# Layer 0 attention: paired maxima on row halves, and a step's values behind all its scores; layer 1's values at the end of the step

## The reference, cut to what matters

```python
# layer 0: 16 query heads of 64, 4 key/value heads, causal
q = (hidden_states @ Wq.T).reshape(B, S, 16, 64).transpose(0, 2, 1, 3)
k = (hidden_states @ Wk.T).reshape(B, S, 4, 64).transpose(0, 2, 1, 3)
v = (hidden_states @ Wv.T).reshape(B, S, 4, 64).transpose(0, 2, 1, 3)
k = jnp.repeat(k, 4, axis=1); v = jnp.repeat(v, 4, axis=1)
scores = jnp.einsum("bhqd,bhkd->bhqk", q, k) * scale + causal
probs = jax.nn.softmax(scores, axis=-1)
out = jnp.einsum("bhqk,bhkd->bhqd", probs, v)
return out.transpose(0, 2, 1, 3).reshape(B, S, 16 * 64) @ Wo.T
# layer 1's second attention: the same shape of work with 16 heads of 8, after a norm and rope
```

## Time and profile before

| | us |
|---|---|
| runs, median of 3 | 1522.89 (1521.58 to 1523.54) |
| the profiled execution | 1521.91 |
| its span, first to last instruction | 1520.2 |
| attention 64 | 43 to 640 |
| attention 8 | about 1006 to 1318 |

### The profile page before, as it was taken

One profiled execution on the slowest core, in us unless ns is written; L12 is line 12 of the kernel. 1 busy time (PEld: TensorE's weight loads), 2 busy tenths in 40 slices (PEclk: granted clock), 3 DMA queues, 4 the chain that ended last, 5 costly groups with the idle time before them and its releaser, 6 DMA issues. The chain is left out here.

```text
span 1520.2 us, 21410 instructions
## 1 busy us (share of the span) xinstructions
PE 1325.6 (87%) x7772; PEld 762.8 (50%) x7772; DVE 969.0 (64%) x1750; ACT 696.5 (46%) x1319; POOL 112.6 (7%) x155
## 2 busy tenths in 40 slices
PE   4689999999999999868999967337989888889998
PEld 3344444444444444346888845313334333256886
DVE  4556545454546462177999966748767655357998
ACT  2242434333333433244666654412665556525664
POOL 0000000101010101000000000302111111020000
PEclk9799999999999999959999979656999888868999
DMA  3101202020201110006676610041212210102221
GB/s 104 40 15 34 49 15 63 8 58 15 52 15 43 29 29 16 14 15 144 146 154 153 146 24 1 2 100 54 47 48 49 53 40 20 43 21 79 78 102 28
DMA packets 51475, 81.61 MB, mean 54 GB/s; under 512 B 16748, under 2 KB 34452, under 8 KB 47444
## 3 DMA queue, kind: packets, MB, share of 16 engines
q1 hardware_dynamic: 51004, 79.40, 21.2%
q10 hardware_dynamic: 384, 1.05, 0.6%
HBM read 63.75 MB, written 5.68 MB: 46 GB/s over the span
## 5 line engine op out<-in xcount | busy, mean ns | idle before, releaser
L1345 PE MATMUL ps<-qA 128*128 128x512 f32 x960 | 252.3, 399 | 15.3 <-POOL qA L1455 10.9
L634 DVE TENSOR_REDUCE mraw<-ps 128x1 f32<-128x512 f32 (+3 forms) x304 | 186.8, 656 | 108.7 <-PE ps L516 60.2
L736 ACT ACTIVATE shared<-ps 128x512 f32<-128x512 f32 (+1 forms) x216 | 121.3, 566 | 261.4 <-PE ps L549 259.8
L1062 DVE TENSOR_REDUCE mraw<-ps 128x2 f32<-128x1024 f32 (+3 forms) x160 | 173.5, 1114 | 78.0 <-PE ps L967 52.3
L1117 ACT ACTIVATE shared<-ps 128x512 f32<-128x512 f32 (+2 forms) x320 | 155.7, 560 | 136.6 <-PE ps L983 136.0
L1345 PEld LDWEIGHTS ps<-qA 128*128 128x128 f32 x960 | 182.5, 192 | 62.9 <-POOL qA L1455 12.3
L548 PE MATMUL ps<-qA,kH 128*128 128x512 f32 (+3 forms) x384 | 165.9, 442 | 6.1 <-DMA qB<-mT 5.8
L548 PEld LDWEIGHTS ps<-qA,kH 128*128 128x128 f32 x384 | 72.9, 190 | 150.7 <-issue 62.6
L1409 ACT CAST qA<-shared 128x512 fp32r<-128x512 f32 x160 | 99.3, 621 | 88.6 <-DVE shared L1547 87.0
L1357 PE MATMUL ps<-qA,kH 128*128 128x512 f32 x480 | 136.3, 393 | 4.0 <-DVE qA L1471 4.0
L549 PE MATMUL ps<-qB,kL 65*128 65x512 f32 (+3 forms) x384 | 130.5, 350 | 0.0
(11 more groups left out here) (247 smaller groups left out, 1755.2 us busy)
## 6 DMA issues: line engine op xcount, KB each, us to landing
shared<-comb SPq DMA_DIRECT2D x92, 256.0 KB, 4.3
qB<-qA SPq DMA_DIRECT2D x16, 512.0 KB, 4.8
rB<-a0rec_dram SPq DMA_DIRECT2D x60, 128.0 KB, 2.8
shared<-comb SPq DMA_DIRECT2D x7, 1024.0 KB, 4.4
rB<-a1rec_dram SPq DMA_DIRECT2D x28, 128.0 KB, 2.7
e0wUp<-in_w SPq DMA_DIRECT2D x48, 64.0 KB, 4.5
qA<-q_split SPq DMA_DIRECT2D x24, 128.0 KB
q_split<-qA SPq DMA_DIRECT2D x4, 512.0 KB
```

Of the source, the lines that this page charges most:

```text
L634: nc.vector.tensor_reduce(out[:, h0:h0 + n_h, qt % 4], src, AX, ALU.max).then_inc(w_free, 1)
L736: nc.scalar.activation(probs(n)[:, hs[0]:hs[-1] + 1, lo:512], src, ACT.Exp, scale=scale)\
L1062: nc.vector.tensor_reduce(out[:, :, js[0]:js[-1] + 1, qt % 4], src, AX, ALU.max).then_inc(x_free, 1)
L1345: ins = nc.tensor.matmul(bank[0:M, :], w[par][:, at:at + M], h[:, cols], start=(r == 0), stop=(r == 2))
```

## The change

1. `max` jobs come in pairs. The query heads' high parts and remainders are written so that even heads have the high part in rows 0 to 63 of `qA` and odd heads in rows 64 to 127. A pair is two matmuls of 64 rows each, on the two halves of the rows, into two banks: only the high part of the queries takes part in the maxima. Masks follow, one for each bank, on all 128 rows. Jobs of 128 and 256 keys are now two jobs (two heads each) instead of one or two, so a group has 40 maxima jobs instead of 38, in 20 pairs. A pair enters when the job three before its second has been released.
2. The planner moves a pair as one, with weight 2.
3. A step's three rounds of values stand as one block behind all its scores and jobs.
4. `copy_q` is two DMAs, one for the even and one for the odd heads.
5. In attention 8, `values` stands at the end of every step.

```diff
     def max_jobs_of(qc):
...
-                n = 512 // keys_in(qt, ch)
-                out += [(qt, ch, h, n) for h in range(0, REP, n)]
+                if keys_in(qt, ch) <= 256:
+                    out += [(qt, ch, i, (i, i + 2)) for i in range(2)]
+                else:
+                    out += [(qt, ch, h % 2, (h,)) for h in range(REP)]
...
-        weights = [3 if job[0] == "proj" else 1 for job in jobs]
+        weights = [{"proj": 3, "max": 2}.get(job[0], 1) for job in jobs]
...
-        opens = m % NU in (0, 4)
+        behind = k - 1
...
-            upto = 3 if i == k - 1 else (i if opens else i + 1)
-            since = 0 if i == 0 else (i - 1 if opens else i)
-            rounds = range(min(since, 3), min(upto, 3)) if m >= 0 else ()
+            rounds = range(3) if m >= 0 and i == behind else ()
...
+                def maxima(pair):
...
+                    if pair[1] >= JOB_BANKS:
+                        pe.wait_ge(w_free, pair[1] - JOB_BANKS + 1)
...
+                    for slot, h in enumerate(evens):
+                        for i in range(2):
+                            half = slice(i * hd, (i + 1) * hd)
+                            ins = nc.tensor.matmul(k.bank(pair[i] % JOB_BANKS)[:, slot * width:(slot + 1) * width],
+                                                   k.qA[par][half, h + i, qt * P:(qt + 1) * P],
+                                                   k.kH[par][half, ch * 512:ch * 512 + width], start=(slot == 0),
+                                                   stop=not diagonal, skip_group_check=True)
...
-                    sp.dma_start(k.qB[g % 2][0:hd, :, cols].bitcast(F32), k.qA[g % 2][0:hd, :, cols].bitcast(F32))\
-                        .then_inc(qb_ld[qc], 16)
+                    for i in range(2):
+                        sp.dma_start(k.qB[g % 2][0:hd, i::2, cols].bitcast(F32),
+                                     k.qA[g % 2][i * hd:(i + 1) * hd, i::2, cols].bitcast(F32)).then_inc(qb_ld[qc], 16)
...
-                    between = n >= LAG and len(jobs) == 4 and (n - LAG) % NU not in (0, 4)
...
-                        if at == 1 and between:
-                            values(n - LAG)
-                    if n >= LAG and not between:
+                    if n >= LAG:
                         values(n - LAG)
```

More of the change, by code:

```diff
@@ L489, in _, with job @@
             def _(pe):
-                def job(idx):
+                def maxima(pair):
+                    kind, g, qc, j = JOBS[pair[0]]
+                    par = g % 2
+                    if pair[1] >= JOB_BANKS:
+                        pe.wait_ge(w_free, pair[1] - JOB_BANKS + 1)
+                    if j == 0:
+                        pe.wait_ge(w_free, index["proj", g, qc, U - 1] + 1)
+                    qt, ch, _, evens = MAXES[qc][j]
+                    width = keys_in(qt, ch)
+                    diagonal = ch * 512 + width == (qt + 1) * P
+                    n_h = len(evens)
+                    for slot, h in enumerate(evens):
[5 more added lines that the diff above has]
+                                                   stop=not diagonal, skip_group_check=True)
+                            if not diagonal and slot == n_h - 1:
+                                ins.then_inc(w_full, 1)
+                    if diagonal:
+                        for i in range(2):
+                            ends = k.bank(pair[i] % JOB_BANKS)[:, 0:n_h * width]\
+                                .rearrange("p (h w) -> p h w", w=width)[:, :, width - P:width]
+                            nc.tensor.matmul(ends, k.ident_bf[:, :], k.masks[:, 1:2, :].broadcast_to((P, n_h, P)),
+                                             start=False, stop=True, skip_group_check=True).then_inc(w_full, 1)
+                def job(group):
+                    if len(group) == 2:
+                        maxima(group)
+                        return
+                    idx = group[0]
                     kind, g, qc, j = JOBS[idx]
@@ L502, in job @@
                                          start=True, stop=True).then_inc(w_full, 1)
[L503 to L519, removed]
                     elif kind == "turn":
@@ L581, in values @@
                         ins.then_inc(pv_done, 1)
-                for idx in due[-1]:
-                    job(idx)
+                for group in due[-1]:
+                    job(group)
                 for n in range(STEPS + LAG):
@@ L588, in _ @@
                             scores(n, first_score[n] + at, hs)
-                        for idx in fills:
-                            job(idx)
+                        for group in fills:
+                            job(group)
                         for r in rounds:
@@ L596, in _ @@
                                      stop=True).then_inc(spread_full, 1)
[L597 removed]
+                job((index["fin", G - 1, 1, 0],))
             @block.vector
@@ L670, in normalise @@
                         .then_inc(on_done, 1)
-                for idx in due[-1]:
-                    take(idx)
+                for group in due[-1]:
+                    for idx in group:
+                        take(idx)
                 for n in range(STEPS + LAG):
@@ L681, in _ @@
                         (recips if at == 7 else normalise)(n // NU, 0)
-                    for idx in due.get(n, []):
-                        take(idx)
+                    for group in due.get(n, []):
+                        for idx in group:
+                            take(idx)
                 cols = slice(512, 1024)
@@ L818, in _ @@
                 load_out(1)
-                for idx in due[-1]:
-                    follow(idx)
+                for group in due[-1]:
+                    for idx in group:
+                        follow(idx)
                 for n in range(STEPS + LAG):
```

46 lines of the change are left out of this document (26 added, 20 removed).

## The result

| | before | after |
|---|---|---|
| runs, median (us) | 1523.21 (1521.58 to 1523.54) | 1546.78 (1541.94 to 1554.61) |
| ratio after to before | | 1.0162, 95% interval 1.0119 to 1.0205 |
| profiled execution, its span | 1521.9, 1520.2 | 1546.4, 1544.7 |
| first score of attention 64 | 57.0 | 60.9 |
| first group | 92.1 | 102.9 |

The changed kernel is 1.6% slower: 23.6 us by the medians, 24.5 by the two spans. The starts of a group's first score, and for the end the start of the matmul named, give the table, and they place the difference. Attention 64 is 35.1 us longer (start +3.9, first group +10.8, six steady groups +22.1, last group -1.8), attention 8 is 7.2 us shorter, the stages in between, in which nothing was changed, are 3.7 us shorter, and what follows attention 8 is 0.3 us longer.

The account below looks back on a forecast made before the run. TensorE's own queue was taken to bound layer 0's attention. From 1522 us, +20 for that stage and +10 for the clock gave 1552, put at 1550; range 1507 to 1570, likeliest case 1543 to 1562.

Parts of the forecast that it names:

- Item 5: Steps 4 and 5 of a steady group: second pair waits 1.7 us each on the projection's chain; +3.4 us a group.
- Item 6: Steps 6 to 9: pairs wait 0.2 to 0.3 us on the previous pair's reduce; +1.8 us a group.
- Items 1 to 4: TensorE's work in a steady group: values block -4.2, halved maxima -4.5, row-half visits +7.0, masks +0.1; -1.6 us.
- Item 8: Layer 0's attention: TensorE's clock falls behind half of 13 long waits; +10 us, bounds 0 and 22.
- The first group: First group of layer 0's attention: VectorE bounds its start and loses 0.3 us at each pair with masks; +3 us.
- item 7: Scores behind scores: in the last group the third head waits some 0.4 us in eight steps; +3.3 against -4.5.
- Item 9: Layer 1's attention: values move behind the fourth head in seven of 12 steps; 0 us, bounds -4 and +4.
- The chain doesn't bite: Rival: TensorE reaches the second pair no sooner than VectorE frees its bank; about 1507 us, chance 0.24.
- Pairs don't overlap: Rival: paired maxima don't overlap in layer 0's attention; +4.5 us a group, 1568 us; 0.08 shared with the every-wait clock fall.
- The half shape is free: Rival: row-half visits cost nothing but waits grow; +0.5 us a group, 1525 us, 1532 with the clock; chance 0.08.
- The clock holds: Rival: TensorE's clock doesn't fall behind the new waits; 1541 us, chance 0.17.
- falls each time: Rival: the clock falls at each long wait, or more than once; 1565 us; 0.08 shared with non-overlapping pairs.

Follow-up runs that it names:

- the block alone: Kernel before with only layer 0's three values rounds as one block behind a step's scores and jobs; 1498.21 us, ratio 0.9848.
- full-row experiment: The whole change, but each maxima matmul of a pair works on all 128 rows instead of a row half; 1544.92 us, ratio 1.0153.
- short reduces: The whole change, but VectorE takes the maximum over only the first 64 keys of each head and block; 1508.68 us, ratio 0.9929.
- the two values blocks: Kernel before with layer 0's values as one block and attention 8's values at each step's end, without paired maxima; 1486.23 us, ratio 0.9784.
- projections earlier: The whole change, with the last two projections of a group moved ahead by one pair or two; 1542.65 us, ratio 1.0125.
- the block behind the third head: The whole change, with layer 0's values block one head earlier, between a step's second-last and last head; 1547.67 us, ratio 1.0189.
- the pairs alone: The whole change, but values rounds go back between the heads and attention 8 is as before; 1561.59 us, ratio 1.0267.

## Why the prediction came out right, point by point

The forecast of 1550 us stands against a measured 1546.8, and the mechanism is the one that was named: pairs wait for VectorE. Taken by its terms, it is right partly because errors of opposite sign met.

- **Item 5, the chain from a projection to the second pair.** Right in place and size. Computed: the second pair starts 4.30 us (in step 5, with 512 columns, 4.43) after the projection and waits 1.7 us, in steps 4 and 5. Measured: 4.30 us (183.20 to 187.50) and 4.44, waits of 1.69 and 1.76. Before, with rounds between, the same engines kept the same pace and TensorE came later.
- **Item 6, pair after pair.** Right in total, but not in its parts. By the distances between starts, four pairs in steps 7 and 8 wait 0.18 us each (computed 0.2) and those of step 9 0.26 and 0.28 (computed 0.3); the one behind the copies of the sums waits 0.78 instead of 0.35. Items 5 and 6 were 5.2 us a group; by the distances between matmuls' starts they are about 5.5 (5.1 by TensorE's idle time, so the next item's figures are good to some 0.4 us).
- **Items 1 to 4, the work.** Computed -1.6 us a group, measured 1.5 - 5.5 = -4.0. The block is near its term (3.8 of 4.2). The pairs' own work, which I had at +2.6, came out at about -0.2, and this is the term that was mis-sized. A visit is as priced: a pair of 512 columns is followed by the next matmul after 0.43 us, where 0.23 is its own work (the pair at 199.04 by the scores at 199.48), entry takes 0.10, and the first wide score after it 0.32 (185.09 to 185.41) instead of 0.23. What was wrong is what these replaced. Summed over one group, the scores' first matmuls and the projections reach the next matmul in 16.6 us in the change and 16.9 in the block alone: scores behind a mask or a block were late already, so the 1.4 us for late wide weights (0.8 and 0.6) is no new cost. And the maxima with their masks took 13.3 us in the block alone, not the 9.0 and 1 that I counted, since they too paid for changes of shape and short waits; in the change they take 10.7, and 12.7 with the 20 entries of 0.10 in front of them. I halved a term that was too small. The Trainium skill, "TensorEngine Tiling (Array Packing)", Key Properties, has the change of mode drain the array. The trace agrees in that a visit has a price: 0.10 on entry, 0.20 for the first pair and the exit. The twofold speed that the same page of the Trainium skill gives in its table of theoretical speedups is there too: the two matmuls of a pair mostly start 3 to 4 ns apart. By the full-row experiment the price of the visits and the halved columns cancel.
- **The steady group.** I called it 73.0 us, by dividing the 438 us window by six; the groups before are 71.54 apart, and the window holds a little more than six. Nothing in the sum went by it, but the sign to look for (76 instead of 73) was off: at full clock it is 73.0 instead of 71.5, +1.5 and not +3.
- **Item 8, the clock.** Right in kind, and larger. In the six steady groups there are twelve waits of the chain, and behind six of them the clock falls. Half was taken without a row for it, between bounds of none and all, so that it came out is luck. The length of a fall was misread: of the three stretches in attention 8 that were said to look the same, the third lasts 6.8 us and not 3.4, in the trace of before already, and two of the six falls here last 10.2. A window of before, and two of the change:

```profile
1261.20:1268.00 6.80, 6.54 (x39) 3.47 (x37) 3.14 (x3) 4.84 (x10) 0.00 (x0) 0.50 0.30 81
...
343.80:354.00 10.20, 10.20 (x35) 4.65 (x27) 5.76 (x12) 2.97 (x5) 0.00 (x0) 0.50 0.11 25
422.30:432.50 10.20, 10.20 (x23) 4.31 (x23) 5.26 (x11) 2.93 (x5) 0.00 (x0) 0.50 0.08 19
```

  The five groups with a fall are 13.2 us longer together than five like the first, for 34 us of low clock: +13, where item 8 had 10 with the first group in it. +9 from the work and waits and +13 from the clock make the +22, where the sum had 18 and 10.
- **The first group.** The step that failed. It was +3, and start and first group together are +14.7. Windows of the change from 46.8 on:

```profile
46.80:67.30 20.50, 12.38 (x34) 5.83 (x34) 7.45 (x15) 2.64 (x5) 0.00 (x0) 0.50 0.04 12
70.70:94.60 23.90, 20.23 (x70) 9.68 (x74) 15.68 (x26) 3.75 (x7) 1.90 (x3) 0.50 0.11 26
```

  It has 37.1 us of low clock instead of 9.6. I priced VectorE's lost time and gave the clock one wait here, though the earlier trace rows and the page had shown a start below full clock already. With full rows the group has 20.6 us of low clock and takes 97.1; with short reduces it has 32.1 and takes 94.3. An estimate: at the 0.34 to 0.47 us that a microsecond of low clock costs in the steady groups (last section), the 27.5 us more would be 9 to 13, all of the 10.8 by which this group is longer. But short reduces alone take 8.6 us off it and only 5.0 us of low clock. Both the clock and VectorE's reduces are in it, and these runs don't split them.
- **The last group and item 7.** -1 computed, -1.8 measured.
- **Item 9, attention 8.** 0 with bounds of 4 us either way, and -7.2 measured. The work is as said: nothing. The clock was the bound's reason, and it was put too narrow. The prediction had named more than 4 us here as a sign that it is wrong, and this sign was met. The experiment with this part alone shows that the gain belongs to it and is no accident of the run; what in the clock brings it stays open.
- **The rivals.** *The chain doesn't bite* fell with the measured wait. *Pairs don't overlap* fell with 3 to 4 ns. *The half shape is free* fell with the 0.43 us a pair. *The clock holds* and *falls each time* fell with six falls in twelve. Against the sum of +30, start and first group came out 11.7 us dearer, the steady groups with all of item 8 set against them 5.9 cheaper, the last group 0.8 cheaper, attention 8 7.2, and the unchanged stages 3.4. That leaves 24.4, the difference of the two spans. So what start and first group cost beyond their term was balanced by four smaller items, two of which, attention 8 and the unchanged stages (10.6 us), I had not forecast: that the sum came this near is in part luck.

## What to carry to other kernels

When work is taken from between two instructions that share a buffer, add up the chain that frees the buffer (projection, copy, remainder, reduce) and set it against what is left in the queue: the 1.7 us wait was readable from the trace of before, and here such waits and the clock behind them were dearer than what the move saved. Cut such a change into its parts: the two values blocks gain 34.6 us together, and the pairs give back more than that. On a queue that is never idle, price an added wait with the clock behind it too, since that was more than half of the loss in the steady groups (13 of 22 us).

## What the runs showed of the hardware

- The clock fell behind waits that were shorter than I had looked for: of 1.31 us with every steady group falling (projections earlier), of 0.84 and 0.20 us in one group of the block behind the third head, and of 0.71 and 0.20 us in one group of the pairs alone. It did not fall behind waits of 1.69 and 1.76 in one group of the change, nor behind those of 1.36 and 1.30 in four of six groups of the short reduces. In the kernel before and in the block alone, with 0.4 us at most, no steady group has low clock. No run here isolates what decides it.
- A microsecond at 1.2 GHz costs 0.34 to 0.47 us where TensorE is the bound: 3.5 us for 10.2 and 5.0 for 13.7 in the change, 1.6 for 3.4 and 4.6 for 10.2 with short reduces. I had taken 0.5. In the two groups of the change with 10.2 us in one stretch the wait of 0.78 in step 6 is gone and TensorE idles for 4.5 us instead of 5.4: under the low clock it comes later to the bank. That is about half of the difference there; the rest was not looked into.
- Halving the columns of the maxima on row halves and paying 0.3 us a visit for it came out even: 1546.8 against 1544.9 us. With two matmuls in most visits the halves did not pay here.
